# A wait of GpSimd in a softmax attention layer that begins at the 128th tile in place of the 320th

## The reference, cut to what matters

```
e = a_src[src] + a_dst[dst]
e = jnp.where(e > 0, e, SLOPE * e)
m = jax.ops.segment_max(e, dst, num_segments=n)
e = jnp.exp(e - m[dst])
s = jax.ops.segment_sum(e, dst, num_segments=n)
alpha = e / (s[dst] + SM_EPS)
msg = alpha[:, :, None] * h[src]
out = jax.ops.segment_sum(msg, dst, num_segments=n)
```

## Time and profile before

| | us |
|---|---|
| median of 3 runs | 5527.91 |
| lowest and highest of the runs | 5525.43, 5542.02 |
| span of the profiled execution | 5821.8 |
| `attend3` in it, first to last gather (L1740) | 4076.3 to 5381.2 |

### The profile page before, as it was taken

One profiled execution on the slowest core, in us unless ns is written; L12 is line 12 of the kernel. 1 busy time (PEld: TensorE's weight loads), 2 busy tenths in 40 slices (PEclk: granted clock), 3 DMA queues, 4 the chain that ended last, 5 costly groups with the idle time before them and its releaser, 6 DMA issues. The chain is left out here.

```text
span 5821.8 us, 59032 instructions
## 1 busy us (share of the span) xinstructions
PE 3339.7 (57%) x14332; PEld 2165.0 (37%) x14332; DVE 3534.5 (61%) x6569; ACT 2187.4 (38%) x3989; POOL 2214.4 (38%) x2086
## 2 busy tenths in 40 slices
PE   5666679999999999789034332333000443433565
PEld 3555534444444444456032332333000443333452
DVE  6999989999999999310134332333211664545676
ACT  4999967878788887200000000000000111111210
POOL 0000023333333333000666777772777056666200
PEclk8999989999999999899556555555555555555556
DMA  2555544444444443787321422212111012111011
GB/s 74 163 162 162 162 131 114 119 111 111 119 109 116 116 115 97 155 187 157 57 45 38 92 47 43 50 34 22 35 28 33 9 33 36 31 36 30 5 36 35
DMA packets 546254, 474.35 MB, mean 81 GB/s; under 512 B 185774, under 2 KB 439737, under 8 KB 545086
## 3 DMA queue, kind: packets, MB, share of 16 engines
q1 hardware_dynamic: 493723, 416.13, 28.5%
q0 software_dynamic: 52288, 55.34, 5.9%
HBM read 351.39 MB, written 119.84 MB: 81 GB/s over the span
## 5 line engine op out<-in xcount | busy, mean ns | idle before, releaser
L815 PE MATMUL l_sum_ps<-arena,sums 125*65 125x500 f32 (+1 forms) x2600 | 1144.6, 578 | 9.9 <-ACT arena L776 4.8
L1740 POOL DMA_INDIRECT l_rows<-table,tile_src x782 | 768.9, 983 | 521.1 <-issue 232.6
L1143 POOL DMA_INDIRECT l_rows<-hidden_rows,tile_src x782 | 794.9, 1017 | 341.8 <-issue 231.5
L694 POOL COPY arena<-arena 125x750 f32<-125x750 f32 (+1 forms) x400 | 538.9, 1351 | 894.6 <-PE l_count_ps L804 864.9
L760 ACT ACTIVATE arena<-arena,far_left 125x750 f32<-125x750 f32 (+1 forms) x800 | 713.3, 939 | 285.7 <-DVE arena L713 285.7
L713 DVE SCALAR_TENSOR_TENSOR arena<-arena,far_past 125x750 f32<-125x750 f32 (+1 forms) x800 | 807.1, 1055 | 16.1 <-DMA arena<-score_rows 16.1
L1204 PE MATMUL l_sum_ps<-l_rows,l_hot 128*125 x1612 | 360.1, 414 | 768.6 <-issue 651.9
L724 DVE SCALAR_TENSOR_TENSOR arena<-arena,l_count_ps 125x750 f32<-125x750 f32 (+1 forms) x800 | 739.4, 970 | 100.5 <-ACT arena L765 52.0
L1934 PE MATMUL l_sum_ps<-l_rows,l_hot 128*128 x1962 | 483.6, 424 | 439.3 <-issue 268.9
L1170 DVE TENSOR_TENSOR sums<-sums,l_sum_ps 125x64 f32 x806 | 178.6, 222 | 777.9 <-DMA arena<-counts 485.6
L1204 PEld LDWEIGHTS l_sum_ps<-l_rows,l_hot 128*125 128x125 f32 x1612 | 341.3, 322 | 787.7 <-issue 786.9
(11 more groups left out here) (440 smaller groups left out, 3021.8 us busy)
## 6 DMA issues: line engine op xcount, KB each, us to landing
arena<-counts SPq DMA_DIRECT2D x300, 328.1 KB
counts<-arena SPq DMA_DIRECT2D x324, 284.4 KB
arena<-counts SPq DMA_DIRECT2D x17, 2843.8 KB
arena<-counts SPq DMA_DIRECT2D x100, 382.8 KB
l_attr<-edge_attr_in SPq DMA_DIRECT2D x97, 256.0 KB
arena<-score_rows SPq DMA_DIRECT2D x24, 732.4 KB
l_rows<-hidden_rows,tile_src POOLq DMA_INDIRECT x782
l_rows<-table,tile_src POOLq DMA_INDIRECT x782
```

The lines of the kernel that those rows point to most:

```text
L694: g.tensor_copy(laid[k % 2][:, 0:n * P].rearrange("p (b v d) -> p b v d", b=n, d=D), raw[k % RAWS][:, 0:n * P].rearrange("p (v b d) -> p b ...
L815: last = nc.tensor.matmul(sum_ps[0:F + 1, c, 0:hi - lo], h_one[:, w, :], z[k % ZS][:, lo:hi], start=(w == 0), stop=(w == W - 1))
L1143: pool.indirect_dma_start(rows[:, b % RING, t, :], None, m.hidden_rows[:, :], bass.IndirectOffsetOnAxis(ap=m.tile_src[:, k:k + 1], axis=0) ...
L1740: pool.indirect_dma_start(rows[:, t % RING3, :], None, m.table3[:, :], bass.IndirectOffsetOnAxis(ap=m.tile_src[:, t:t + 1], axis=0)).then_ ...
```

## The change

One bound is changed. The wait for `sums_ready` begins at tile 128 (2 x `PART`) in place of 320 (`RING3`). Its formula stays.

```diff
-                if t >= RING3 and t % 8 == 0:
+                if t >= 2 * PART and t % 8 == 0:
                     pool.wait_ge(sums_ready, (t + 7 - RING3 + NW - 1) // STEPS + 1)
```

## The result

| | before | changed |
|---|---|---|
| median, us (18 runs each) | 5527.51 | 5541.95 |
| lowest to highest | 5523.14 to 5543.66 | 5528.62 to 5555.62 |
| ratio | | 1.0025 (1.0017 to 1.0033) |

A forecast was written before the change was run, and what follows sets the result against it. The prediction took GpSimd's gathers to bound the edge stage. Three newly throttled parts at 7 us each gave 21 us: 5527.9 + 21 = 5549 us, 0.4% slower, own range 5540 to 5561, with rival 2 and run spread 5524 to 5569.

The forecast's parts named there:

- the band that it had named as the sign of too high a price: Timed runs of the changed kernel within 5520 to 5540 us would show the price of a throttled part too high.
- GpSimd bounds the stage, and each microsecond it loses arrives at the end: Edge stage: PE waits for gathers at every turn down to part 11, so GpSimd's lost time delays the end.
- Three parts are newly throttled: Tiles 128 to 319: parts 2, 3 and 4 run throttled in place of free; 17 to 31 us in all.
- The price of a throttled part: GpSimd's gathers: what a throttled part of 64 tiles costs more than a free one, taken as 7 us.
- lower bound: 5.6 us a part: 3.5 us of wait behind the turn and 2.1 us for four longer landing pauses.
- upper bound: 10.5 us a part: throttled part of 97.2 us less free part of 86.7 us, both from the trace.
- The stalls are in the profiled execution and not in the timed ones: Gather stretches of the first trace: 287 to 292 us of stalls assigned to profiling, absent from timed runs.
- The account by stretches: Stalls of 154 to 159, 104 (third layer) and 29 us; 5821.8 - 290 = 5532 us for the kernel before.
- The first rival: Between turns of parts 1 and 5 the stalls are real: 104 to 124 us faster, 5404 to 5424 us; chance 0.10.
- The second: New gates cost nothing measurable; only longer landing pauses are left, 6 us, 5534 us; chance 0.08.
- the third rival: Throttled start settles worse, with second pauses and a longer first gate: 52 us, 5580 us; chance 0.03.
- The span of the changed kernel: Profiled execution gets shorter by about 100 to 125 us, to some 5700 to 5720 us, while timed runs get longer.

The follow-up runs named there:

- free chips: Chips 3 and 12 (second and third series), one series each; the kernel before, run beside each edit, took 5524.66 and 5523.81 us there.
- the clean trace of the kernel before: Kernel before run again in the second series, no edit but one constant written in another form: 5526.6 us, ratio 1.0001, span 5523.3.
- crawling chip: Chips 15 and 13 (first and fourth series), one series each; the kernel before, run beside each edit, took 5826.62 and 5804.89 us there.

## Why the prediction was right, and where it was wrong

It said 5549 us, slower by 0.4%, with a range of its own of 5540 to 5561. The runs gave 5541.95, slower by 0.25%. That is inside the range, but by the prediction's own line of 0.3% it is "same", to which it gave 0.33, and not "slower", to which it gave 0.57. The later runs of the changed kernel on free chips, 5537.8 and 5534.92, fall into the band that it had named as the sign of too high a price.

- **GpSimd bounds the stage, and each microsecond it loses arrives at the end**: right, though it was read from a trace with the crawl, in which the turn of part 7 has no such wait. In the clean trace of the kernel before PE waits 32 to 36 us for gathers at every turn from part 2 to part 11. Between the turns of parts 1 and 4 the three clean traces of the changed kernel need 282.8, 283.0 and 285.3 us against 272.4, so 10.4 to 12.8 us more, and the timed runs 12 to 14 us more.
- **Three parts are newly throttled, the gate of tile 128 is open, the first wait stands before tile 136 and takes some 4 us**: right, 3.85 us.
- **The price of a throttled part**: mis-sized. I took 7 us, from bounds of 5.6 and 10.5. The clean traces give 3.5 to 4.3 (10.4 to 12.8 over three parts), the timed runs 4 to 5 (12 to 14 us over three), all below my lower bound. In the upper bound the free part of 86.7 us failed. I read it where the other engines stood still; where they work it is 90.8, since landing pauses average 1.92 us there and not 1.73, and the work of 64 gathers is 64.9 us (194.6 / 3) and not 61.8. The throttled part is 94.3 to 95 us and not 97.2: that term held 2.5 us of crawl. In the lower bound the wait of 3.5 us behind a turn was right. The landing pauses cost 1.4 us a part and not 2.1 ((24.9 + 2.2 - 23.0) / 3), and a term was missing: the gathers' own work falls by 1.6 us a part, which I had taken as equal in both kernels. These two nearly cancel, so the wait behind the turn is nearly the whole price in the traces.
- **The stalls are in the profiled execution and not in the timed ones**: right for the runs that were to be predicted, wrong as the general statement that I made. All timed runs of two series crawl (5802 to 5842 us in the first). The step that failed is the inference from "the span is 294 us above the median" to "the profiling does it". It could as well be another condition of the machine, as the two series have it; on which chip the first profile was taken isn't on record. The idle machine in the earlier trace rows doesn't show that timed runs are without the stalls. The account by stretches, 5532 us for a run without stalls, came close to the 5526.6 measured, but in part by luck. Against the clean trace the first one loses 104 us before the turn of part 1 (I had 104, for the third layer), 145 between the turns of parts 1 and 5 (154 to 159), 17 from there to the turn of part 12 (29), and 32 behind it, where I had nothing: GpSimd issues 32 more indirect gathers there (L1745).
- **The first rival**: I gave it a chance of 0.10 and a price of 104 to 124 us. It is what happens on a crawling chip, 123 us, with 391 us for the four parts where it had 389; the first gate that costs up to 20 us did not come (GpSimd stood 7.7 us before tile 128 and 2.0 before tile 136). Which condition the runs would meet was not in the trace. It was in their median: 5527.91 us is near the account without the stalls, and far from any with them. That is why the direction came out right. The second and the third rival did not come: the waits behind the turns last 3.85 us, and no part costs 14 us.
- **The span of the changed kernel**: I expected 5700 to 5720 and it is 5546.0 on a free chip, 5675.9 on a crawling one. The forecast mixed the two: it counted on a crawling profile. That crawl stays in the third layer and in the later parts, where the change does nothing.

The Trainium skill's page "Runtime: NRT & Kernel Launch" ("The ~15µs preamble/postamble breakdown") holds that a profile's total stands a near constant 6.2 µs above the reported time. I set it aside because of the 294 us. For that profile the time of the same execution isn't on record. In every other run that has both, the span from the first to the last instruction stands some 2 us *below* the time (5546.0 and 5548.2). So the 6.2 is not what these rows show, but what the rule makes of a gap of 294 us, that it is not the profile's addition, was the better guide. The backpressure of "NOTIFIC — the notification-queue block", section 7.1, is neither shown nor excluded.

**What stays open** is what makes a chip crawl. It was seen on chips 13 and 15 and not on 3 and 12, and within a series it did not change. No run tells chip from session. All timed runs of the series carry spans and clocks, so a recording that holds the engines on some chips, in timed runs too, remains a rival that nothing here tests.

## What to carry to other kernels

When the profiled span and the timed median differ by more than a fraction of a per cent, the profile may come from another condition of the machine than the times. Take a second profile of the same program before pricing anything with the first, and price a stretch only by stretches in which the same engines are at work. A throttle on a producer costs what it adds to that producer's stream, here 3.5 to 5 us a part, when the producer is the bound. It can give some ten times that back (41 us a part here) where the producer's rush slows the consumers. A change like this should be timed on more than one chip.

## What the runs showed of the hardware

Beside GpSimd's indirect gathers, on two of the four chips of the series, DVE, PE and ACT slow down. Beside its other work they do not: the first gather of the third layer stands at 2795 to 2808 us in every trace, crawling or free, and GpSimd makes 400 copies (L694) before it. Nor is it the clock or the instructions themselves: the granted clock is 0.50 in this stretch in both conditions, and the matmuls of the sums have the same median of 417 ns. The view of ACT's copies (L1981) has its register instructions (instances: shortest / median / longest ns), first from the kernel before on the crawling chip, then on the free one:

```profile
L1981 ACTq FUSED_REGOPS  x1377: 3/64/1608, 4189.8 to 5576.1; - x197
```

```profile
L1981 ACTq FUSED_REGOPS  x1377: 42/64/175, 4085.2 to 5283.7; - x197
```

A register instruction takes up to 1.6 us there, while its median is the same. PE's longest at L1934 is 926 ns against 171. DVE's stay at 57 ns, but DVE stands 358.7 us in 29 waits before L1855 that the view puts down to a DMA for which that line doesn't wait; on the free chip it has no such wait. So the engines are held between instructions and in register instructions; what holds them no row shows. On the crawling chip ACT's copies start 1.40 us apart, or twice that:

```profile
4516.59 0.21 ACT L1981 ACTIVATE l_step_att<-l_att 128x8 f32 x1 [2.59 <-issue]
4517.99 0.21 ACT L1981 ACTIVATE l_step_att<-l_att 128x8 f32 x1 [1.19 <-issue]
4519.39 0.21 ACT L1981 ACTIVATE l_step_att<-l_att 128x8 f32 x1 [1.19 <-issue]
```

A pace so even looks like something handed out at a fixed rate, which is a guess. After the last gather has ended, this lasts another 11 us with no gather running:

```profile
4513.96:4524.70 10.74, 0.00 (x0) 0.00 (x0) 0.00 (x0) 1.28 (x7) 0.00 (x0) 0.50 0.01 3
```

PE, DVE and GpSimd have no instruction in it and the DMA share is 0.01. And when GpSimd really waits for the sums, the others keep up: 16 groups of sums per 97 us in place of 292.
